# A slot-attention and mixture-of-experts kernel: scores ahead of the query turn, the slot sums' reciprocal behind the subtraction, four groups written out

## The chip, the cores and the metric

One core of a Trainium2 chip runs the whole kernel. The metric is the device time of one execution in microseconds (us). The engines are TensorE (PE; its weight loads are listed as PEld), VectorE (DVE), ScalarE (ACT), GpSimd (POOL) and SyncE (SP, which here only issues DMAs). Each engine runs its own list of instructions in order and waits for the others at semaphores.

## The reference

Cut to what matters. `x` is 32 batches of 56 slots with 128 features, `ctx` is 32 batches of 1500 tokens with 128 features.

```python
slots = layernorm(x)
Pn = rmsnorm(ctx, input_norm_w); k = Pn @ Wk.T; v = Pn @ Wv.T
for _ in range(3):
    q = rmsnorm(slots, slot_norm_w) @ Wq.T
    scores = einsum('bkd,bmd->bkm', q, k) * SCALE
    attn = softmax(scores, axis=-2)                      # over the 56 slots
    attn = attn / (attn.sum(-1, keepdims=True) + EPS)    # over the 1500 tokens
    slots = gru_cell(attn @ v, slots)
x = x + slots
x = x + top2_of_8_experts(layernorm(x))                  # each expert: gelu(x @ w1.T) @ w2.T
```

## The kernel before

The 32 batches are worked on in four groups of eight (`PAIR = 8`, `NPAIR = 4`). For a group there is an attention stage and then an expert stage. In the expert stage the context of the next group is also loaded, normalized, split into two fp16 parts (`ctx_rows`) and turned (`ctx_cols`). Ahead of the first group stands a prologue that does this for group 1, with the weights.

The attention stage has 24 steps (three iterations of eight batches), laid over 28 rounds (`ROUNDS`), n = 0 to 27. A step s is one batch in one iteration. Its work is spread over rounds:

- PE makes the scores of step n + 1 in round n (`scores`, L418: 12 chunks of 125 tokens by 3 products, 36 matmuls into one of two pairs of PSUM banks), and in round n the attention-weighted sums of step n - 3 (`update`, L431 and L436).
- DVE in round n takes the maximum over the slots of step n (L985), sums the exponentials of step n - 1 (L992), scales these sums (L1007) and takes their reciprocal `rden` (L1010), and then subtracts the maximum of step n from its scores (L1016), which is what ACT needs for the exponential of step n (L688).
- POOL multiplies the exponentials of step n - 1 with `rden` (L813). ACT casts the result of step n - 2 to fp16 (L674) and POOL makes the low half (L807), after which PE can run `update`.

Every second round one couple of batches (112 slots) also passes through the gated unit. In even rounds DVE normalizes the sums (L1030, L1033) and PE runs the gates (L457). In odd rounds ACT makes the gates (L663, L668) and the candidate (L684), DVE combines them (L999, L1003, L1021, L1027) into the new slots `h`. In even rounds the new slots make queries: ACT squares them (L608), PE forms the sum of squares and the query rows (`queries`, L399 and L400), ACT and POOL make the scale (L612, L772) and scale the rows (L617), and PE turns them (`turn_q`, L405). ACT and DVE write the two halves of the turned query, `qk` (L622, L890). The scores of an even step wait for that.

On PE a round of before has this order: `gates_of_slots` (L449), `queries`, `update`, `turn_q`, `scores`, then a slots' turn at the end of the stage, and `gates_of_updates` (L457). In rounds 0 to 2 there is no `update` yet.

In every engine's program a loop (`Fori`) runs the body for groups 1 to 3, and the body stands a second time for group 4, which has no next context to prepare. The loop's back edge is taken twice, at the end of groups 1 and 2. The last thing that PE does in a body of the loop is `scores` of step 0 of the next group, and a wait for the experts' last sum (`mixed`). SP's body begins with the loads of the next group's first three contexts and ends with the store of the group's output.

Of the kernel before, what the change touches and what calls it, by code (L numbers as in the profile page):

```python
# [14 lines left out]
TP = 125  # L15
TPE = TP + 1
CHUNKS = TOKENS // TP
# [33 lines left out]
def slot_attention_moe(nc, x, ctx, wq, wk, wv, wih, whh, bih, bhh, slot_w, input_w, router, w1, w2, out):  # L51
    with ExitStack() as stack:
# [227 lines left out]
        def _(sp):  # L280
            def load_ctx(j, b):
                r = b % RAW
                src = ctx[batch_of(j, b):batch_of(j, b) + 1] if isinstance(j, int) else ctx[bass.ds(batch_of(j, b), 1)]
                src = src.rearrange("o (p c) d -> p (o c) d", c=CHUNKS)

                if b >= RAW:
                    wait(sp, rows_ready, nth(j, PAIR, b - RAW + 1))
                elif not (isinstance(j, int) and j == 0):
                    wait(sp, rows_ready, nth(j, PAIR, b + RAW * (raw_uses(b) - 1) + 1 - PAIR))
                sp.dma_start(ctx_raw[0:XDMA_ROWS, r], src[0:XDMA_ROWS]).then_inc(ctx_loaded[r], DMA)  # L290
                sp.dma_start(ctx_raw[XDMA_ROWS:TP, r], src[XDMA_ROWS:TP]).then_inc(ctx_loaded[r], DMA)
# [4 lines left out]
            def rows_of(t, j):  # L296
                j8 = t[j * PAIR:(j + 1) * PAIR] if isinstance(j, int) else t[bass.ds(j * PAIR, PAIR)]
                return j8.rearrange("(t b) k d -> (b k) t d", b=2)

# [48 lines left out]

            with sp.Fori(0, NPAIR - 1) as i:
                body(i, True)  # L350
            body(NPAIR - 1, False)
            sp.wait_ge(out_stored, DMA * (NPAIR + 1))
# [3 lines left out]
        def _(pe):  # L356
# [50 lines left out]
            def scores(i, s):  # L407
                b, g = s % PAIR, (s // GROUP) % NG
                if s % GROUP == 0:
                    wait(pe, qk_ready, nth(i, GSTEPS, s // GROUP + 1))  # L410
                if s < PAIR:
                    wait(pe, cols_by_dve, nth(i, PAIR, b + 1))
                    wait(pe, cols_by_act, nth(i, 2 * PAIR, 2 * (b + 1)))
                wait_reuse(pe, shift_ready, i, STEPS, s - 1)
                for c in range(CHUNKS):
                    o = (c % HALF) * SLOTS
                    for n, (cp, qp) in enumerate(PRODUCTS):
                        mm = pe.matmul(score_ps[:, 2 * (s % 2) + c // HALF, o:o + SLOTS], ctx_cols[:, b, cp, c, :],  # L418
                                       qk[:, g, qp, (b % GROUP) * SLOTS:(b % GROUP + 1) * SLOTS],
                                       start=(n == 0), stop=(n == 2))  # L420
                mm.then_inc(scores_ready, 1)
# [104 lines left out]
            def body(i, more):  # L526
                for n in range(ROUNDS):
# [5 lines left out]
                    if LAG <= n < STEPS + LAG:  # L533
                        update(i, n - LAG)
                    if m is not None:
                        turn_q(i, m)
                    if n + 1 < STEPS:
                        scores(i, n + 1)
                    if tile_done_at(n) is not None and tile_done_at(n) < RT - 1:
# [35 lines left out]

            with pe.Fori(0, NPAIR - 1) as i:
                body(i, True)
            body(NPAIR - 1, False)

# [4 lines left out]
        def _(act):  # L584
# [151 lines left out]

            with act.Fori(0, NPAIR - 1) as i:
                body(i, True)
            body(NPAIR - 1, False)


        @block.gpsimd
        def _(pool):
# [83 lines left out]

            with pool.Fori(0, NPAIR - 1) as i:
                body(i, True)
            body(NPAIR - 1, False)  # L830


        @block.vector
        def _(dve):
# [142 lines left out]
            def body(i, more):  # L977
                chain.enter(PRO + i * PER)
                for n in range(ROUNDS):
# [15 lines left out]
                    if done is not None:  # L995
# [8 lines left out]
                            .then_inc(npre_ready, 1)  # L1004
                    if 0 <= s < STEPS:
                        wait(dve, den_ready, nth(i, STEPS, s + 1))
                        nc.vector.tensor_scalar(dup_ps, den_ps, 1.0 / ATTN_UP, None, ALU.mult).then_inc(den_scaled, 1)  # L1007
                        wait(dve, den_scaled, nth(i, STEPS, s + 1))
                        wait_reuse(dve, soft_ready, i, STEPS, s - 1)
                        nc.vector.reciprocal(rden[0:TP, s % 2], dup_ps).then_inc(rden_ready, 1)  # L1010
                    if n < STEPS:
# [4 lines left out]
                        nc.vector.tensor_tensor(soft[0:TP, n % 4].rearrange("p (h c) k -> p h c k", h=2), banks,  # L1016
                                                tops, ALU.subtract).then_inc(shift_ready, 1)
                    if done is not None:

# [4 lines left out]
                    if done is not None:  # L1024
                        wait(dve, cand_scaled, nth(i, GSTEPS, done + 1))
                        wait(dve, zh_ready, nth(i, GSTEPS, done + 1))
                        nc.vector.tensor_tensor(h[:, done % NG, :], zh[:, :], z_cand_home(done), ALU.subtract).then_inc(h_ready, 1)  # L1027
                    if gs is not None:
                        wait(dve, upd_ready, nth(i, STEPS, GROUP * (gs + 1)))
# [52 lines left out]

            with dve.Fori(0, NPAIR - 1) as i:
                body(i, True)
            body(NPAIR - 1, False)


# [24 lines left out]
```

## Time and profile before

| | us |
|---|---|
| median of 3 runs | 862.6 |
| lowest and highest run | 862.13 and 865.19 |
| profiled execution | 859.8 |
| its span, first to last instruction | 857.9 |
| prologue | 0 to 79.5 |
| attention rounds, group 1 | 79.5 to about 195 |
| first maximum (L985) of groups 2, 3 and 4 at | 282.3, 491.4, 697.3 |

How to read the rows: times are us from the start of the span. A line of the timeline has the start, the duration, the engine, the line of the kernel, the operation, output and inputs, and how many instructions were merged. In square brackets stands how long the engine was idle before it, and who released it; "issue" there means that nothing the profile shows was waited for. Within one engine, an instruction can start a little before the one ahead of it has ended.

### The profile page before, as it was taken

To read this page: it belongs to the slowest core of one execution; us is meant where nothing else is said; L and a number is where in the kernel's file an instruction comes from. 1 tells how busy PE (TensorE), PEld (TensorE's weight loads), DVE (VectorE), ACT (ScalarE), POOL (GpSimd) and SP (SyncE) were. 2 spreads that over 40 slices of the span, in tenths; PEclk is the share of its full clock that TensorE was granted. 3 is DMA by queue.
4 is the path that set the end of the run, shared out by engine and by line. 5 is a ranking of instruction groups with operands and counts; after the bars stand their busy time and mean duration, and the time that the engine had idled before them with its cause. 6 is when DMAs were issued, how large, how long until landed. Compare 5 with 4: busy or idle time off the path is not lost.

```text
span 857.9 us, 31055 instructions
## 1 busy us (share of the span) xinstructions
PE 662.3 (77%) x12876; PEld 571.3 (67%) x12876; DVE 685.1 (80%) x1406; ACT 526.1 (61%) x1048; POOL 529.2 (62%) x446
## 2 busy tenths in 40 slices
PE   2656899958676499985767569998676859998697
PEld 1545899845555499984556569997364659998476
DVE  5786899977986499996979559998697869999476
ACT  3664566648676256664858436666576755666375
POOL 5973787884574177878465237888565717787300
PEclk9767799988998599998989869999698989999799
DMA  8754000001310400000221130000031100000000
GB/s 176 182 146 134 3 4 3 4 12 42 102 41 2 122 3 4 3 4 11 74 72 38 38 85 4 3 5 3 12 108 37 38 12 3 5 3 3 2 2 12
DMA packets 15456, 33.45 MB, mean 39 GB/s; under 512 B 1411, under 2 KB 10259, under 8 KB 15307
## 3 DMA queue, kind: packets, MB, share of 16 engines
q1 hardware_dynamic: 15307, 31.36, 14.0%
q8 instruction: 107, 1.75, 0.8%
q14 instruction: 42, 0.34, 0.1%
HBM read 30.29 MB, written 0.92 MB: 36 GB/s over the span
## 4 chain that ended last, share of the span: by engine, by line
issue 31%; PE 25%; POOL 20%; DVE 18%; ACT 4%; DMA 2%; SPq 1%; POOLq 0%; ACTq 0%; DVEq 0%
POOL ctx_raw L755 8%; POOL ctx_rstd L753 7%; PE score_ps L418 5%; PE upd_ps L431 5%; DVE soft L1016 4%; DVE score_ps L992 3%; PE upd_ps L436 3%; PE score_ps L478 3%; PE score_ps L465 2%; DVE top L985 2%; PE gru_ps L399 2%; PE gru_ps L400 2%; DVE qk L890 1%; POOL attn L807 1%; DMA soft<-in_L_ffn_w_dram 1%
## 5 line engine op out<-in xcount | busy, mean ns | idle before, releaser
L807 POOL TENSOR_TENSOR attn<-soft,attn 125x672 f16<-125x672 f32 x96 | 140.6, 1464 | 29.5 <-ACT attn L674 28.6
L478 PEld LDWEIGHTS score_ps<-w_t,hidden 128*128 128x128 f16 x1536 | 103.6, 104 | 59.4 <-DVE hidden L1052 37.3
L813 POOL TENSOR_TENSOR soft<-soft,rden 125x672 f32<-125x672 f32 x96 | 126.0, 1312 | 24.3 <-DVE rden L1010 24.3
L478 PE MATMUL score_ps<-w_t,hidden 128*128 128x128 f16 x1536 | 116.8, 231 | 28.9 <-DVE hidden L1052 28.9
L1052 DVE TENSOR_TENSOR hidden<-hid,hidden 128x448 f16<-128x448 f32 x128 | 99.4, 785 | 48.2 <-ACT hidden L702 47.6
L418 PE MATMUL score_ps<-qk,ctx_cols 128*128 128x56 f16 x3456 | 113.5, 192 | 10.5 <-DVE qk L890 5.6
L755 POOL TENSOR_TENSOR ctx_raw<-ctx_raw,ctx_rstd 125x1536 f32<-125x1536 f32 x32 | 116.9, 3652 | 2.5
L418 PEld LDWEIGHTS score_ps<-qk,ctx_cols 128*128 128x128 f16 x3456 | 106.4, 99 | 12.6 <-issue 9.8
L985 DVE TENSOR_REDUCE top<-score_ps 125x12 f32<-125x672 f32 x96 | 81.9, 853 | 38.7 <-PE score_ps L418 33.6
L431 PE MATMUL upd_ps<-attn,ctx_rows 126*128 126x56 f16 x3456 | 108.1, 189 | 3.3 <-POOL attn L807 3.0
L465 PE MATMUL score_ps<-ycols,w_t 128*128 128x448 f16 x384 | 105.4, 393 | 5.1 <-ACT hid L707 5.1
L431 PEld LDWEIGHTS upd_ps<-attn,ctx_rows 126*128 126x128 f16 x3456 | 105.4, 97 | 5.5 <-POOL attn L807 4.9
L688 ACT ACTIVATE soft<-soft 125x672 f32<-125x672 f32 x96 | 73.2, 762 | 52.9 <-DVE soft L1016 50.4
L370 PE MATMUL upd_ps<-ident,ctx_rows 128*128 128x128 f16 x768 | 70.5, 250 | 43.1 <-DVE ctx_rows L847 30.0
L370 PEld LDWEIGHTS upd_ps<-ident,ctx_rows 128*128 128x128 f16 x768 | 56.7, 114 | 51.8 <-issue 19.4
L992 DVE TENSOR_REDUCE score_ps<-soft 125x12 f32<-125x672 f32 x96 | 81.7, 851 | 1.5 <-ACT soft L688 1.4
L674 ACT CAST attn<-soft 125x672 f16<-125x672 f32 x96 | 71.5, 744 | 16.4 <-POOL soft L813 14.4
L593 ACT CAST ctx_rows<-ctx_raw 125x1536 f16<-125x1536 f32 x32 | 47.3, 1478 | 51.3 <-POOL ctx_raw L755 51.3
L707 ACT ACTIVATE hid<-score_ps 128x448 f32<-128x448 f32 x128 | 69.7, 548 | 12.6 <-PE score_ps L465 12.3
L1016 DVE TENSOR_TENSOR soft<-score_ps,top 125x672 f32<-125x672 f32 x96 | 76.8, 800 | 0.5
L436 PE MATMUL upd_ps<-attn,ones 126*128 126x56 f16 x2304 | 76.5, 188 | 0.0
L753 POOL TENSOR_TENSOR ctx_rstd<-ctx_ms,mhalf 125x12 f32<-125x12 f32 x32 | 72.7, 2272 | 2.6 <-POOL ctx_ms L752 0.2
(127 smaller groups left out, 1220.1 us busy)
## 6 DMA issues: line engine op xcount, KB each, us to landing
ctx_raw<-in_ctx_dram SPq DMA_DIRECT2D x32, 672.0 KB
soft<-in_L_ffn_w_dram SPq DMA_DIRECT2D x16, 256.0 KB, 5.0
ctx_raw<-in_ctx_dram SPq DMA_DIRECT2D x32, 78.0 KB
x_in<-in_x_dram SPq DMA_DIRECT2D x4, 224.0 KB, 2.7
out_dram<-acc SPq DMA_DIRECT2D x4, 224.0 KB, 3.2
soft<-in_L_xattn_gru_wih_dram SPq DMA_DIRECT2D x1, 192.0 KB, 3.6
soft<-in_L_xattn_gru_whh_dram SPq DMA_DIRECT2D x1, 192.0 KB, 3.8
ctx_rows<-hidden SPq DMA_DIRECT2D x1, 144.0 KB
```

The source lines that it names most:

```text
L370: mm = pe.transpose(bank[:, k * D:(k + 1) * D], ctx_rows[:, b, part, c, :], ident16[:, :])
L418: mm = pe.matmul(score_ps[:, 2 * (s % 2) + c // HALF, o:o + SLOTS], ctx_cols[:, b, cp, c, :], qk[:, g, qp, (b % GROUP) * SLOTS:(b % GROUP ...
L431: pe.matmul(upd_ps[:, gs % 2, o:o + SLOTS], ctx_rows[0:TPE, b, cp, c, :], attn[0:TPE, s % 3, ap, c, :], start=(c == 0 and n == 0), stop=(c ...
L436: mm = pe.matmul(upd_ps[:, gs % 2, GW + o:GW + o + SLOTS], ones16[0:TPE, :], attn[0:TPE, s % 3, ap, c, :], start=(c == 0 and ap == HI), st ...
L465: mm = pe.matmul(score_ps[:, n % 2, 0:PW], w1_t[:, wp, e, c * D:(c + 1) * D], ycols16[:, yp, :], start=(k == 0), stop=(k == 2))
L478: mm = pe.matmul(score_ps[:, 2 + e % 2, t * D:(t + 1) * D], hidden[:, n % HRING, hp, t * ROWS:t * ROWS + D], w2_t[:, wp, e, c * D:(c + 1) ...
L753: chain.link(nc.gpsimd.tensor_tensor(ctx_rstd[0:TP, r], ctx_ms[0:TP, r], mhalf[0:TP, :], ALU.pow))
L755: nc.gpsimd.tensor_tensor(rows, rows, ctx_rstd[0:TP, r].unsqueeze(2).to_broadcast([TP, CHUNKS, D]), ALU.mult).then_inc(ctx_scaled, 1)
L807: nc.gpsimd.tensor_tensor(attn[0:TP, s % 3, LO], soft[0:TP, s % 4], attn[0:TP, s % 3, HI], ALU.subtract).then_inc(attn_ready, 1)
L813: nc.gpsimd.tensor_tensor(a, a, rden[0:TP, s % 2].unsqueeze(2).to_broadcast([TP, CHUNKS, SLOTS]), ALU.mult).then_inc(soft_ready, 1)
L992: nc.vector.tensor_reduce(den_ps, soft[0:TP, s % 4], AX_X, ALU.add).then_inc(den_ready, 1)
L1016: nc.vector.tensor_tensor(soft[0:TP, n % 4].rearrange("p (h c) k -> p h c k", h=2), banks, tops, ALU.subtract).then_inc(shift_ready, 1)
```

## The change

Three edits.

- The loops over the groups are written out: each engine's body is emitted four times with constant addresses and semaphore values.
- On PE, `scores` of step n + 1 is issued ahead of `turn_q`, behind `update`. For steps 3 and up `scores` now waits for `rden_ready` of step s - 3 and not for `shift_ready` of step s - 2. Both come from DVE's round s - 2, where the reciprocal now stands behind the subtraction, and the reciprocal's input lies in the same pair of banks.
- On DVE, the subtraction L1016 goes ahead of the scaling L1007 and of the reciprocal L1010. The scaling follows right behind it, and the reciprocal stands behind the two operations that finish the slots (L1021, L1027).

```diff
@@ PE, scores
-                wait_reuse(pe, shift_ready, i, STEPS, s - 1)
+                if s >= 3:
+                    wait(pe, rden_ready, nth(i, STEPS, s - 2))
+                else:
+                    wait_reuse(pe, shift_ready, i, STEPS, s - 1)
@@ PE, round
+                    if n + 1 < STEPS:
+                        scores(i, n + 1)
                     if m is not None:
                         turn_q(i, m)
-                    if n + 1 < STEPS:
-                        scores(i, n + 1)
@@ DVE, round
-                    if 0 <= s < STEPS:
-                        wait(dve, den_ready, nth(i, STEPS, s + 1))
-                        nc.vector.tensor_scalar(dup_ps, den_ps, 1.0 / ATTN_UP, None, ALU.mult).then_inc(den_scaled, 1)
-                        wait(dve, den_scaled, nth(i, STEPS, s + 1))
-                        wait_reuse(dve, soft_ready, i, STEPS, s - 1)
-                        nc.vector.reciprocal(rden[0:TP, s % 2], dup_ps).then_inc(rden_ready, 1)
                     if n < STEPS:
...
                                                 tops, ALU.subtract).then_inc(shift_ready, 1)
+                    if 0 <= s < STEPS:
+                        wait(dve, den_ready, nth(i, STEPS, s + 1))
+                        nc.vector.tensor_scalar(dup_ps, den_ps, 1.0 / ATTN_UP, None, ALU.mult).then_inc(den_scaled, 1)
                     if done is not None:
...
                         nc.vector.tensor_tensor(h[:, done % NG, :], zh[:, :], z_cand_home(done), ALU.subtract).then_inc(h_ready, 1)
+                    if 0 <= s < STEPS:
+                        wait(dve, den_scaled, nth(i, STEPS, s + 1))
+                        wait_reuse(dve, soft_ready, i, STEPS, s - 1)
+                        nc.vector.reciprocal(rden[0:TP, s % 2], dup_ps).then_inc(rden_ready, 1)
@@ every engine (here PE)
-            with pe.Fori(0, NPAIR - 1) as i:
-                body(i, True)
-            body(NPAIR - 1, False)
+            for i in range(NPAIR):
+                body(i, i < NPAIR - 1)
```

## Rows read from the trace of the kernel before

**Rows 1.** The page: busy time by engine, and a DMA queue (packets, MB).

```profile
PE 662.3 (77%) x12876; PEld 571.3 (67%) x12876; DVE 685.1 (80%) x1406; ACT 526.1 (61%) x1048; POOL 529.2 (62%) x446
q8 instruction: 107, 1.75, 0.8%
```

**Rows 2.** Stretches: length, busy time per engine (PE, PEld, DVE, ACT, POOL), clock, DMA share, GB/s.

```profile
79.50:100.00 20.50, 15.45 (x321) 14.26 (x320) 14.22 (x26) 8.94 (x20) 10.16 (x10) 0.67 0.13 37
282.30:308.50 26.20, 16.13 (x321) 14.77 (x321) 14.19 (x26) 9.23 (x21) 10.13 (x10) 0.61 0.36 93
491.40:516.50 25.10, 15.90 (x322) 14.65 (x322) 14.26 (x27) 9.24 (x21) 10.22 (x10) 0.66 0.36 95
697.30:716.30 19.00, 12.66 (x321) 11.69 (x321) 14.25 (x27) 8.75 (x20) 10.13 (x10) 0.91 0.05 14
...
107.50:155.40 47.90, 45.73 (x1274) 43.55 (x1269) 45.91 (x105) 31.92 (x79) 39.04 (x38) 1.00 0.01 4
```

**Rows 3.** Timeline of DVE: an odd round's maximum, then the next odd round.

```profile
108.02 0.86 DVE L985 TENSOR_REDUCE top<-score_ps 125x12 f32<-125x672 f32 x1
...
115.80 0.85 DVE L985 TENSOR_REDUCE top<-score_ps 125x12 f32<-125x672 f32 x1
...
118.10 0.17 DVE L1007 TENSOR_SCALAR score_ps<-score_ps 125x12 f32<-125x12 f32 x1
...
118.30 0.23 DVE L1010 RECIPROCAL rden<-score_ps 125x12 f32<-125x12 f32 x1
118.45 0.79 DVE L1016 TENSOR_TENSOR soft<-score_ps,top 125x672 f32<-125x672 f32 x1
...
119.16 0.27 DVE L1021 SCALAR_TENSOR_TENSOR upd_ps<-z_gate,upd_ps 128x112 f32<-128x112 f32 x1
...
119.46 0.27 DVE L1027 TENSOR_TENSOR h<-zh,upd_ps 128x112 f32<-128x112 f32 x1
```

**Rows 4.** Timeline of PE and DVE at the end of the next, even, round.

```profile
121.72 0.78 PE L436 MATMUL upd_ps<-attn,ones 126*128 126x56 f16 x24
...
122.48 0.32 PE L405 MATMUL gru_ps<-ident,q_rows 112*128 112x112 f32 x1
...
122.63 1.09 PE L418 MATMUL score_ps<-qk,ctx_cols 128*128 128x56 f16 x36
...
123.43 0.27 DVE L1033 TENSOR_TENSOR upd<-upd_ps,inv_sum 128x112 f32<-128x112 f32 x1
...
123.76 0.92 PE L457 MATMUL gru_ps<-upd,wx_t 128*128 128x112 f32 x6
123.77 0.86 DVE L985 TENSOR_REDUCE top<-score_ps 125x12 f32<-125x672 f32 x1
```

**Rows 5.** Timeline of ACT and POOL between the two.

```profile
118.47 0.35 ACT L684 ACTIVATE upd_ps<-npre,vec 128x112 f32<-128x112 f32 x1
118.64 1.46 POOL L807 TENSOR_TENSOR attn<-soft,attn 125x672 f16<-125x672 f32 x1 [0.22 <-ACT attn L674]
...
119.95 0.28 ACT L608 ACTIVATE h_sq<-h 128x112 f32<-128x112 f32 x1
120.06 1.31 POOL L813 TENSOR_TENSOR soft<-soft,rden 125x672 f32<-125x672 f32 x1
```

**Rows 6.** Timeline of PE across the back edge into group 2.

```profile
279.71 1.09 PE L418 MATMUL score_ps<-qk,ctx_cols 128*128 128x56 f16 x36
284.70 0.53 PE L399 MATMUL gru_ps<-ones,h_sq 128*112 128x1 f32 x2 [3.89 <-issue]
...
291.15 1.00 PE L418 MATMUL score_ps<-qk,ctx_cols 128*128 128x56 f16 x18 [2.64 <-issue]
```

**Rows 7.** Timeline of the first rounds of group 4: a turn, two maxima.

```profile
699.22 0.31 PE L405 MATMUL gru_ps<-ident,q_rows 112*128 112x112 f32 x1 [1.38 <-ACT q_rows L617]
...
700.51 0.86 DVE L985 TENSOR_REDUCE top<-score_ps 125x12 f32<-125x672 f32 x1 [1.49 <-PE score_ps L418]
...
708.82 0.86 DVE L985 TENSOR_REDUCE top<-score_ps 125x12 f32<-125x672 f32 x1 [2.37 <-PE score_ps L418]
```

More of the change, by code:

```diff
@@ L282, in load_ctx @@
                 r = b % RAW
-                src = ctx[batch_of(j, b):batch_of(j, b) + 1] if isinstance(j, int) else ctx[bass.ds(batch_of(j, b), 1)]
-                src = src.rearrange("o (p c) d -> p (o c) d", c=CHUNKS)
+                src = ctx[batch_of(j, b):batch_of(j, b) + 1].rearrange("o (p c) d -> p (o c) d", c=CHUNKS)
                 if b >= RAW:
                     wait(sp, rows_ready, nth(j, PAIR, b - RAW + 1))
-                elif not (isinstance(j, int) and j == 0):
+                elif j > 0:
                     wait(sp, rows_ready, nth(j, PAIR, b + RAW * (raw_uses(b) - 1) + 1 - PAIR))
@@ L296, in rows_of @@
             def rows_of(t, j):
-                j8 = t[j * PAIR:(j + 1) * PAIR] if isinstance(j, int) else t[bass.ds(j * PAIR, PAIR)]
-                return j8.rearrange("(t b) k d -> (b k) t d", b=2)
+                return t[j * PAIR:(j + 1) * PAIR].rearrange("(t b) k d -> (b k) t d", b=2)
             load_ctx(0, 0)
@@ L347, in body @@
                 sp.dma_start(rows_of(out, i), acc[:]).then_inc(out_stored, DMA)
-            with sp.Fori(0, NPAIR - 1) as i:
-                body(i, True)
-            body(NPAIR - 1, False)
+            for i in range(NPAIR):
+                body(i, i < NPAIR - 1)
             sp.wait_ge(out_stored, DMA * (NPAIR + 1))
@@ L574, in body @@
                     wait(pe, mixed, nth(i, EXPERTS, EXPERTS))
-            with pe.Fori(0, NPAIR - 1) as i:
-                body(i, True)
-            body(NPAIR - 1, False)
+            for i in range(NPAIR):
+                body(i, i < NPAIR - 1)
         EXP_TANH = "exp_and_others"
@@ L735, in body @@
                         copy_turned(i + 1, PAIR - 1, t)
-            with act.Fori(0, NPAIR - 1) as i:
-                body(i, True)
-            body(NPAIR - 1, False)
+            for i in range(NPAIR):
+                body(i, i < NPAIR - 1)
         @block.gpsimd
@@ L826, in body @@
                             rstd_rows(nth(i + 1, LNT_PER, RT))
-            with pool.Fori(0, NPAIR - 1) as i:
-                body(i, True)
-            body(NPAIR - 1, False)
+            for i in range(NPAIR):
+                body(i, i < NPAIR - 1)
         @block.vector
@@ L1081, in body @@
                             qk_lo(i + 1, 0)
-            with dve.Fori(0, NPAIR - 1) as i:
-                body(i, True)
-            body(NPAIR - 1, False)
+            for i in range(NPAIR):
+                body(i, i < NPAIR - 1)
 _INS = ['x', 'ctx_1024', 'L0_xattn_Wq', 'L0_xattn_Wk', 'L0_xattn_Wv', 'L0_xattn_gru_wih', 'L0_xattn_gru_whh',
```

## The prediction

> **What bounds the kernel now.** I read the page first, then stretches, then the chain of waits for their order, and the timeline round by round. DVE is the busiest engine over the span [rows 1], but an average over stages decides nothing. In steady attention rounds DVE is busy for 45.91 of 47.90 us, PE for 45.73, POOL for 39.04 and ACT for 31.92, at full granted clock (1.00, which is 2.4 GHz) [rows 2]. DVE and PE are thus both close to full, and what sets the time is a loop through both. The chain of waits passes, for every couple of batches, from DVE's subtraction and the new slots (L1016, L1021, L1027) over ACT's square (L608) to PE's queries, the update (L431, L436) and then either DVE's L1030 and L1033 or PE's turn and scores (L405, L418), to the next maximum L985. Two such turns take from 108.02 to 123.77, so 7.88 us for one pair of rounds [rows 3, 4].
>
> The first rounds of a group are another matter. From the first maximum to the sixth they take 20.50, 26.20, 25.10 and 19.00 us in the four groups, and DVE is busy for only 14.2 of them each time [rows 2]. Two things stand out. In groups 2 and 3, which are entered by the loop's back edge, 6 to 7 us more pass than in group 4, which isn't. And in group 4 too DVE waits for scores that stand behind a query turn [rows 7].
>
> **Part 1, the loops written out.** At the back edge PE has finished its scores at 280.80 (279.71 + 1.09) and begins its next instruction at 284.70, 3.89 us idle of which nothing is released by another engine; within the scores of step 1 it stops again for 2.64 us [rows 6]. With constant addresses there is no jump, so both should go. How much of it reaches the end is best read from whole starts. From the last matmul of the first scores to the sixth maximum, groups 1 and 4, entered straight, need about 20.5 and 19.0 us: the stretches of rows 2 begin within 0.1 us of that matmul. Groups 2 and 3 need their 26.2 and 25.1 plus the 1.5 us (280.80 to 282.30) by which DVE too starts late at the back edge [rows 2, 6]; for group 3 I take the same 1.5. If they become like group 1 the gain is 7.2 + 6.1 = 13.3 us; like group 4, 8.7 + 7.6 = 16.3. Group 4's clock in this stretch is 0.91, against 0.67 in group 1, and its DMAs are few (0.05 against 0.13), while groups 2 and 3 load contexts there (0.36) [rows 2]. I take the middle, 15.
>
> The stop inside the scores could also be put down to those loads and not to the jump. Then the 2.64 us stay in both groups, 5.3 us, and part 1 brings 9.7. The rows lean to the jump, since the stop comes in PE's first matmuls behind it and group 1, which loads as well, shows no such stall in its 20.50 us. The Trainium skill (Runtime: NRT & Kernel Launch, Instruction fetch mechanics) says that instructions are fetched in blocks of 16 KiB one ahead of the other, and that a taken branch to a target outside the two blocks held forces a fetch before execution goes on. By that rule the stop goes too and part 1 is worth its full 15; by the reading from the loads it would be 9.7. The queue's 107 packets of 1.75 MB [rows 1] agree with 16 KiB each.
>
> The longer programs cost nothing that I can find: they execute the same instructions, and in the steady rounds, where nothing is loaded, the DMAs still move 4 GB/s [rows 2], so instructions are being fetched while they run, loop or not. On SP the loads of the next contexts go out about 1 us earlier, with nothing queued that is needed before round 24; should they disturb, it is the 5.3 us above.
>
> **Part 2, scores ahead of the turn, in the first rounds.** In round 0, and in the same way in round 2, PE stands 1.38 us before the turn, waiting for ACT's scaled rows, while the next scores, whose query has long been there, are queued behind it; DVE then waits 1.49 us for the maximum of step 1 and 2.37 us for that of step 3 [rows 7]. Now those scores run in that gap. They need 1.1 us at full clock [rows 4], so the first turn, before at 699.22, is hardly later (scores could start at 697.84, 1.38 ahead, and end at 698.9). Its query is as early as before. The maximum of step 1 comes 1.5 us earlier. With it the subtraction, the exponential and, queued behind that on ACT, the square for the next query come earlier, and in round 2 the wait for the scores of step 3 goes as well: 1.49 + 2.37 = 3.9 us is the most. The turn of step 3's neighbour then lands behind the scores, and update 0 waits for POOL, whose line L813, ACT's cast, L807 starts only with the first reciprocal. That gives some back, about 1 us. The least is 1.5 (only the first gap). I take 2.9 for each group, nearer the top, because both waits have the same cause: 4 x 2.9 = 11.6 us.
>
> **Part 3, steady rounds.** In an odd round L1016 takes the place of L1007 and starts at 118.10, not 118.45. It ends at 118.89. L1007 (0.17, overlapping by 0.08 as independent DVE instructions do here: 118.45 against 118.53) ends at 118.99, L1021 follows from 118.91 and L1027 from 119.21 to 119.48, where it ended at 119.73: 0.25 us earlier, since the 0.23 us reciprocal has left this path [rows 3]. L1021 needs ACT's candidate, ready at 118.82 [rows 5], so it just isn't held. L608 started 0.22 after the slots at 119.95 [rows 5], and PE's queries and update end 0.25 earlier with it, and so do L1030 and L1033. The turn used to stand between L436's end at 122.50 and the scores, which ended at 123.72, just ahead of L985 at 123.77 [rows 4]. With the turn (0.3) behind the scores they end about 0.2 + 0.25 earlier, so DVE's side is the later: L1033 ended at 123.70 and L985 can overlap it by 0.08. It starts 0.25 + 0.15 = 0.40 earlier in this pair of 7.97, and 0.25 in the other of the two, which has 7.78 (15.75 - 7.97) and no wait for scores. That is 0.33 on average, and 7.55 a pair.
>
> Is the moved work covered? The turn now ends at about 123.4 of the old times; L457 behind it waits for L1033 anyway, and ACT's L622 has until DVE has done the next L985. The reciprocal of the odd round ends at about 119.63, against 118.53; behind it waits POOL's L813, which started only at 120.06, held by L807 until 120.10 [rows 5]. The cover is 0.43 us and is what I trust least: if the candidate came later by more than that, L813 would move. The new wait of the scores on `rden_ready` concerns the DVE round before. PE gets to the even round's scores at 122.3, 2.7 us behind that reciprocal. It holds nothing. In even rounds the reciprocal ends as before, 0.1 us sooner.
>
> There are nine such pairs from the sixth maximum to the 24th in each group, so 36 x 0.33 = 12 us. An alternative value comes from the other end: nothing at all if POOL or ACT close the loop in DVE's stead (0), or 0.5 us a pair (18) if scores too drew everything forward. The expert stage and the last four rounds see neither edit: 0.
>
> **Sum.** 15 + 11.6 + 12 = 38.6, say 39 us. From the profiled execution, 859.8 (span 857.9 and 1.9 around it), this leaves 820.8. That execution lies 2.8 us below the median of the runs, 862.6, to which the forecast refers: 862.6 - 39 = 823.6.
>
> **The rivals.**
>
> - The steady rounds don't gain. POOL's multiplication and subtraction (1.31 and 1.46 us [rows 5]) follow each other through ACT's cast, twice a pair, and the late reciprocal uses up its cover. For it: POOL already has 39.04 busy of 47.90 [rows 2], 6.4 us of each pair, with the casts' gaps on top; against it: the 0.43 us of cover. 39 - 12 = 27 gives 835.6.
> - More than forecast: groups 2 and 3 start like group 4, PE's clock stays up in the shorter first rounds, 3.9 us each in part 2 and 0.4 a pair: 16.3 + 15.6 + 14.4 = 46, 816, and down to 810 with 0.5 a pair.
> - Only the loops: the first rounds are given back at once because POOL's line sets the sixth maximum, and the steady rounds stay. 15 alone gives 847.6, and 853 if the stop in the scores stays too.
> - Slower: written out, PE's stream stalls where it runs straight. The place is a block boundary, 107 of them [rows 1], the price that of the stop seen, 2.64 us [rows 6], and it decides from 15 such stops (39 / 2.64). With 25 it would be 890. Against it: the loop's body is itself a long straight line, and in its steady rounds PE is busy 45.73 of 47.90 [rows 2].
> - The change doesn't do what it says: PE has its weight load ahead and gains nothing by the swap. It is part of the third rival, since the 1.38 us before the turn is a real wait for ACT.
>
> **How the numbers follow.** Forecast, 817 to 831: 0.55. Steady rounds without gain, 831 to 843: 0.20. More than forecast, 808 to 817: 0.10. Only the loops, 843 to 858: 0.08. No change: 0.03. Slower: 0.04. The range 809 to 843 leaves out the last three and a little at the bottom, 0.16 to 0.18. A difference under 0.5%, 4.3 us, is about what a measurement of this kernel can't tell from none. Faster 0.93, same 0.03, slower 0.04.
>
> **What would show it.** In the changed kernel PE's idle "issue" of 3.89 and 2.64 us at the starts of groups 2 and 3 is gone (part 1). The first to the sixth maximum take about 16 to 17.5 us in every group (parts 1 and 2), and L418 runs ahead of L405. Pairs of rounds take about 7.55 us, L608 starts 3.9 us after the odd round's L985 and not 4.15, and L813 has no idle time released by L1010 in steady rounds (part 3). The prediction is wrong if L813 shows such waits of over 0.4 us, if pairs stay at 7.8, or if PE's stops for "issue" turn up in the middle of rounds.

## The result and the profile after

The changed kernel takes 824.8 us (median of four runs, 821.59 to 826.13). The runs of before that stand beside it have a median of 863.89. The ratio is 0.953, with a 95% interval of 0.9475 to 0.9586. The forecast was 823.6, in a range of 809 to 843. The profiled execution took 824.36 us with a span of 822.6, which is 35.3 less than the 857.9 of before.

In the changed kernel the maximum is L982, the sum of exponentials L989, the subtraction L1007, the scaling L1011, the reciprocal L1025 and the slots' two operations L1015 and L1021. ACT's candidate is L683 and its square L607, PE's turn is L402, and POOL's two operations are L811 and L805. PE's scores and update keep their lines. First the page: the busy time by engine, and the queue of PE's instructions.

```profile
PE 653.0 (79%) x12876; PEld 565.9 (69%) x12876; DVE 677.9 (82%) x1406; ACT 528.8 (64%) x1048; POOL 522.9 (64%) x446
q8 instruction: 101, 1.65, 0.8%
```

The same work now lies in a shorter span [rows 1]. Next, stretches of the changed kernel, in the columns of rows 2: from the first to the sixth maximum in each group, and steady rounds of group 1.

```profile
80.38:96.12 15.74, 12.17 (x321) 11.24 (x320) 13.86 (x26) 8.51 (x19) 9.34 (x9) 0.89 0.16 44
275.87:292.90 17.03, 13.56 (x321) 12.63 (x321) 13.87 (x27) 8.53 (x20) 10.09 (x10) 0.80 0.58 151
470.49:489.06 18.57, 15.10 (x321) 14.17 (x321) 13.90 (x27) 8.53 (x20) 10.08 (x10) 0.72 0.55 139
665.45:683.83 18.38, 14.91 (x321) 13.97 (x321) 13.90 (x27) 8.53 (x20) 10.09 (x10) 0.72 0.06 15
...
107.50:155.40 47.90, 46.73 (x1336) 45.06 (x1336) 47.02 (x109) 33.64 (x84) 40.79 (x40) 1.00 0.02 4
```

Against [rows 2] the starts are shorter by 4.8, 9.2, 6.5 and 0.6 us. In the steady rounds DVE is now busy for 47.02 of 47.90 us. The starts (from the first to the sixth maximum of a group) get longer as their granted clock falls from 0.89 to 0.72, and PE is busy in them for 12.17 us in the shortest and 15.10 in the longest. Their DVE time is the same in all four.

Now the timeline of one steady odd round, all engines, answering [rows 3] and [rows 5].

```profile
126.23 0.85 DVE L982 TENSOR_REDUCE top<-score_ps 125x12 f32<-125x672 f32 x1
...
128.53 0.85 DVE L1007 TENSOR_TENSOR soft<-score_ps,top 125x672 f32<-125x672 f32 x1
...
128.90 0.35 ACT L683 ACTIVATE upd_ps<-npre,vec 128x112 f32<-128x112 f32 x1
129.07 1.47 POOL L805 TENSOR_TENSOR attn<-soft,attn 125x672 f16<-125x672 f32 x1 [0.21 <-ACT attn L673]
129.29 0.17 DVE L1011 TENSOR_SCALAR score_ps<-score_ps 125x12 f32<-125x12 f32 x1
129.37 0.27 DVE L1015 SCALAR_TENSOR_TENSOR upd_ps<-z_gate,upd_ps 128x112 f32<-128x112 f32 x1
129.41 0.77 ACT L687 ACTIVATE soft<-soft 125x672 f32<-125x672 f32 x1 [0.16 <-DVE soft L1007]
...
129.67 0.27 DVE L1021 TENSOR_TENSOR h<-zh,upd_ps 128x112 f32<-128x112 f32 x1
129.86 0.23 DVE L1025 RECIPROCAL rden<-score_ps 125x12 f32<-125x12 f32 x1
130.00 0.79 DVE L982 TENSOR_REDUCE top<-score_ps 125x12 f32<-125x672 f32 x1
130.08 0.28 ACT L607 ACTIVATE h_sq<-h 128x112 f32<-128x112 f32 x1
...
130.49 1.31 POOL L811 TENSOR_TENSOR soft<-soft,rden 125x672 f32<-125x672 f32 x1
```

ACT's square starts 3.85 us after the odd round's maximum (4.15 before). It stands right behind ACT's exponential L687, which ends at 130.18, and not right behind the slots, which are ready at 129.94. The kernel before has the same order. There the slots were ready at 119.73, but ACT was in its exponential until 120.04, and the square started at 119.95 [rows 5]:

```profile
119.28 0.76 ACT L688 ACTIVATE soft<-soft 125x672 f32<-125x672 f32 x1 [0.46 <-DVE soft L1016]
```

What brings the square forward by 0.30 us is thus the subtraction, which releases the exponential. The reciprocal ends at 130.09 and POOL takes it at 130.49, behind its own L805. The cover is thus 0.40 us and was not used up. The even round that follows, PE and DVE, answers [rows 4].

```profile
131.85 0.78 PE L436 MATMUL upd_ps<-attn,ones 126*128 126x56 f16 x24
...
132.47 1.09 PE L418 MATMUL score_ps<-qk,ctx_cols 128*128 128x56 f16 x36
...
133.41 0.29 PE L402 MATMUL gru_ps<-ident,q_rows 112*128 112x112 f32 x1
133.56 0.27 DVE L1031 TENSOR_TENSOR upd<-upd_ps,inv_sum 128x112 f32<-128x112 f32 x1
133.76 0.85 DVE L982 TENSOR_REDUCE top<-score_ps 125x12 f32<-125x672 f32 x1
```

The scores end at 133.56, ahead of the 133.83 of DVE's L1031, so it is DVE that decides when the next maximum starts. From 126.23 to 133.76 the pair takes 7.53 us.

The table has all kernels that the rest speaks of. "Starts" is the time from first to sixth maximum in groups 1 to 4, "pair" the mean of eight steady pairs (sixth to 22nd maximum) in group 1, with other groups where they differ from it by more than 0.05. Both are read from one profiled execution. A single start can differ by over 1 us where the engines have the same to do: in group 1 it takes 15.7 us in the changed kernel at a clock of 0.89, and 17.2 at 0.80 in e11, where only the loads are moved.

| kernel | median | span | starts, groups 1 to 4 | pair |
|---|---|---|---|---|
| before | 862.6 | 857.9 | 20.5, 26.2, 25.1, 19.0 | 7.89 |
| changed | 824.8 | 822.6 | 15.7, 17.0, 18.6, 18.4 | 7.53 |
| e1 loops written out only | 847.3 | 843.3 | 19.3, 19.3, 19.9, 18.9 | 7.89 |
| e2 both orders, loops kept | 842.8 | 841.5 | 18.2, 25.6, 26.9, 17.2 | 7.52 |
| e3 loops out, PE's order | 840.5 | 832.5 | 17.5, 17.6, 17.8, 17.5 | 7.83 |
| e4 loops out, DVE's order | 837.7 | 837.1 | 20.0, 19.3, 18.2, 20.2 | 7.74 |
| e5 before, late loads | 868.9 (one run) | 867.0 | 20.8, 22.6, 23.0, 19.0 | 8.44, 8.39, 8.44, 7.89 |
| e6 changed, filler | 819.5 | 815.9 | 15.4, 16.0, 17.3, 17.0 | 7.52 |
| e7 changed, reciprocal early | 831.1 | 830.7 | 17.2, 18.5, 17.1, 18.5 | 7.70 |
| e11 changed, loads spaced | 822.9 | 820.8 | 17.2, 17.3, 18.6, 18.4 | 7.53 (group 2: 7.60) |
| e12 changed, loads bunched | 838.1 | 837.1 | 18.2, 17.3, 18.3, 17.2 | 8.00, 8.22, 8.12, 7.52 |
| e8 filler and spaced loads | 820.8 | 816.9 | 15.4, 16.7, 17.0, 16.8 | 7.52 |
| e9 the same, filler in round 3 too | 815.3 | 812.5 | 15.4, 15.4, 15.4, 15.4 | 7.52 (groups 2, 3: 7.63, 7.58) |

Runs of before that shared the chip had medians of 865.2 (e1 to e4), 864.8 (e5 to e7) and 862.1 (e8 to e12).

### The profile page after: what moved, and what is told of

It is laid out like the page before. It is cut to its first block, busy times and chain, and to the rows that moved or that the text cites. A ratio compares the mean times of both kernels' runs of the same rounds, so it can differ in the third digit from the quotient of the medians.

```text
span 822.6 us, 29805 instructions
## 1 busy us (share of the span) xinstructions
PE 653.0 (79%) x12876; PEld 565.9 (69%) x12876; DVE 677.9 (82%) x1406; ACT 528.8 (64%) x1048; POOL 522.9 (64%) x446
## 4 chain that ended last, share of the span: by engine, by line
DVE 47%; PE 19%; issue 13%; POOL 9%; ACT 9%; DMA 2%; SPq 1%; POOLq 0%; DVEq 0%; ACTq 0%
DVE score_ps L989 7%; DVE inv_sum L1028 5%; DVE hidden L1050 4%; PE score_ps L478 4%; DVE soft L1007 4%; DVE top L982 4%; DVE ctx_rows L844 4%; POOL ctx_raw L753 4%; PE score_ps L465 3%; DVE ssq L840 3%; PE upd_ps L367 3%; POOL ctx_rstd L751 2%; DVE rden L1025 2%; PE upd_ps L431 2%; ACT hid L706 2%
## 5 line engine op out<-in xcount | busy, mean ns | idle before, releaser
L805 POOL TENSOR_TENSOR attn<-soft,attn 125x672 f16<-125x672 f32 x96 | 140.6, 1465 | 29.9 <-ACT attn L673 28.9
L1050 DVE TENSOR_TENSOR hidden<-hid,hidden 128x448 f16<-128x448 f32 x128 | 101.1, 801 | 49.1 <-ACT hidden L701 48.8
L811 POOL TENSOR_TENSOR soft<-soft,rden 125x672 f32<-125x672 f32 x96 | 126.1, 1314 | 14.9 <-DVE rden L1025 14.6
L418 PE MATMUL score_ps<-qk,ctx_cols 128*128 128x56 f16 x3456 | 110.0, 190 | 4.1 <-DVE qk L887 3.9
L753 POOL TENSOR_TENSOR ctx_raw<-ctx_raw,ctx_rstd 125x1536 f32<-125x1536 f32 x32 | 110.8, 3463 | 2.5
L418 PEld LDWEIGHTS score_ps<-qk,ctx_cols 128*128 128x128 f16 x3456 | 101.8, 98 | 5.3 <-DVE qk L887 4.6
L982 DVE TENSOR_REDUCE top<-score_ps 125x12 f32<-125x672 f32 x96 | 79.4, 827 | 13.2 <-PE score_ps L418 13.2
L687 ACT ACTIVATE soft<-soft 125x672 f32<-125x672 f32 x96 | 73.1, 762 | 15.4 <-DVE soft L1007 15.4
L989 DVE TENSOR_REDUCE score_ps<-soft 125x12 f32<-125x672 f32 x96 | 81.5, 849 | 0.5
L1007 DVE TENSOR_TENSOR soft<-score_ps,top 125x672 f32<-125x672 f32 x96 | 81.4, 848 | 0.3 <-issue 0.2
```

The lines of the kernel that those rows point to most:

```text
L753: nc.gpsimd.tensor_tensor(rows, rows, ctx_rstd[0:TP, r].unsqueeze(2).to_broadcast([TP, CHUNKS, D]), ALU.mult).then_inc(ctx_scaled, 1)
L805: nc.gpsimd.tensor_tensor(attn[0:TP, s % 3, LO], soft[0:TP, s % 4], attn[0:TP, s % 3, HI], ALU.subtract).then_inc(attn_ready, 1)
L811: nc.gpsimd.tensor_tensor(a, a, rden[0:TP, s % 2].unsqueeze(2).to_broadcast([TP, CHUNKS, SLOTS]), ALU.mult).then_inc(soft_ready, 1)
L982: nc.vector.tensor_reduce(top[0:TP, n % 2], banks, AX_X, ALU.max).then_inc(max_ready, 1)
L989: nc.vector.tensor_reduce(den_ps, soft[0:TP, s % 4], AX_X, ALU.add).then_inc(den_ready, 1)
L1050: nc.vector.tensor_tensor(hidden[:, k % HRING, LO, 0:PW], hid32[:, k % GRING, :], hidden[:, k % HRING, HI, 0:PW], ALU.subtract).then_inc(h ...
```

## The experiments

### Which part brings what: e1 to e4

**e1: the loops written out, nothing else.**

```diff
-            with pe.Fori(0, NPAIR - 1) as i:
-                body(i, True)
-            body(NPAIR - 1, False)
+            for i in range(NPAIR):
+                body(i, i < NPAIR - 1)
```

> The kernel before with only its loops written out; both orders stay. Theory (the back edge costs about 15 us in the starts of groups 2 and 3, nothing elsewhere): first to sixth maximum of groups 2 and 3 at 19 to 20.5 us instead of 26.2 and 25.1, groups 1 and 4 and the steady pairs (7.88 us) unchanged, no idle of 3.89 or 2.64 us for issue; 862.6 - 15 = about 848. Rival A (the stop within the scores comes from the context loads): it stays at 2.6 us in groups 2 and 3, 853. Rival B (the loops are worth more, since the measured starts of the changed group 4 gained only 0.6 us): 840 or less.

Measured: 847.3 us, ratio 0.9797 (0.9766 to 0.9828). The span is 14.6 us shorter than before, pairs are at 7.89, and the starts of groups 2 and 3 are 6.9 and 5.2 us shorter. No stop for issue is left in the starts. That much of the theory holds. Of the 14.6 us, however, only 12.1 lie in the starts of groups 2 and 3. Another 1.6 come from a shorter prologue and 1.2 from the start of group 1, neither of which the back edge touches (in the other kernels with written out loops the first maximum stands at 79.1 to 81.5 us, before it stood at 79.5). The time from the 24th maximum of a group to the next group's first maximum is not shorter: 111.7 and 112.4 us for groups 1 and 2, against 111.5 and 112.1.

**e2: both orders, the loops kept.** The edit is the change's own diff without its last part.

> The changed kernel with the loops kept, so both orders without the writing out. Theory (the parts add up): steady pairs at 7.53 us, 12 us from them, and 2 to 3 us from each start; the stops for issue stay; 862.6 - 12 - 10 = about 840. Rival (behind the back edge PE fetches late, so that scores ahead of the turn gain nothing in groups 2 and 3): 845.

Measured: 842.8, ratio 0.9737 (0.9704 to 0.9769). Pairs are at 7.52, so the whole steady gain comes from the orders. The starts of groups 1 and 4 are shorter than before, but those of groups 2 and 3 are 25.6 and 26.9. Behind the back edge the orders bring nothing. The view of waits tells why:

```profile
PE score_ps L421 <- issue: 10.4, 2, 6.0
PE gru_ps L399 <- issue: 7.4, 2, 3.9
```

These are sum, number and longest. The stop within the first scores, 2.64 us before [rows 6], is now up to 6.0. PE gets to the point sooner, and its instructions are not there sooner. The rival's mechanism was right. Its 845 was not reached, since groups 1 and 4 and the pairs gained.

**e3: loops written out, scores ahead of the turn; DVE as before.**

```diff
-                    if m is not None:
-                        turn_q(i, m)
                     if n + 1 < STEPS:
                         scores(i, n + 1)
+                    if m is not None:
+                        turn_q(i, m)
```

> Loops written out and on PE the scores ahead of the turn, DVE's order as before (reciprocal ahead of the subtraction, scores waiting for the subtraction as before). Theory: the starts gain as in the changed kernel, and of the steady pair only the 0.15 to 0.2 us by which the scores came late in every second pair, so pairs of about 7.78; 4 x 9 x 0.1 = 3.6 of the 12.4 us; about 824.8 + 9 = 834. Rival (DVE's order brings nothing without this one and this one brings all): pairs of 7.53, 825.

Measured: 840.5, ratio 0.9732 (0.9675 to 0.9789), 6.5 above the 834 expected, with runs spread over 11 us. The profiled span of 832.5 lies at the low end of them, so I go by the trace, and what made the other runs longer isn't shown. Starts are 17.5 to 17.8, on average 1.8 us shorter than e1's. Their sum is 70.4, against 69.7 in the changed kernel, so nearly the whole gain of the starts comes from PE's order. Pairs are at 7.83, only 0.06 under e1's, and not at the 7.78 expected.

**e4: loops written out, the subtraction first on DVE; PE as before.** The edit is the change's part on DVE, with the scores' new wait.

> Loops written out and on DVE the subtraction first, the turn still ahead of the scores. Theory: new slots 0.25 us earlier in the odd round, but scores behind the turn then end last: pair 7.97 - 0.25 = 7.72, the starts as in the kernel before (20.5 to 19 us): 848 - 6 = about 842. Rival (the parts don't need each other): pair 7.63.

Measured: 837.7 (842 was expected), ratio 0.9664 (0.9616 to 0.9712). Pairs are at 7.74, against 7.72 expected. Starts are as in e1 (sum 77.7 against 77.5).

Together e3 and e4 say what the change's two orders do in the steady pair. PE's alone brings 0.06 us, DVE's alone 0.15, both 0.36. The two paths into the next maximum (DVE's sums, or PE's turn and scores) end nearly together in the kernel before. Shortening one leaves the other in charge, and only both together give the whole.

### What the place of the reciprocal is worth: e7

```diff
                         nc.vector.tensor_scalar(dup_ps, den_ps, ...).then_inc(den_scaled, 1)
+                        wait(dve, den_scaled, nth(i, STEPS, s + 1))
+                        wait_reuse(dve, soft_ready, i, STEPS, s - 1)
+                        nc.vector.reciprocal(rden[0:TP, s % 2], dup_ps).then_inc(rden_ready, 1)
...
-                    if 0 <= s < STEPS:
-                        wait(dve, den_scaled, nth(i, STEPS, s + 1))
-                        wait_reuse(dve, soft_ready, i, STEPS, s - 1)
-                        nc.vector.reciprocal(rden[0:TP, s % 2], dup_ps).then_inc(rden_ready, 1)
```

> The changed kernel with the reciprocal right behind the scaling, so ahead of the slots' last two operations, both still behind the subtraction. Theory (0.25 us of the pair come from the reciprocal having left the path to the new slots): slots 0.23 us later, ACT's square held by them rather than by its exponential, pair 7.72 to 7.76; 36 x 0.21 = 7.6 us more, 832. Rival (what counts is the subtraction ahead of both, which starts the exponential): pair 7.53 to 7.58, 825 to 827.

Measured: 831.1, ratio 0.9616 (0.9567 to 0.9665), pairs 7.70. In the timeline of e7's odd round the reciprocal (here L1015) stands ahead of the slots (L1019, L1025), and now it is the slots that ACT's square waits for:

```profile
128.17 0.84 DVE L982 TENSOR_REDUCE top<-score_ps 125x12 f32<-125x672 f32 x1
...
131.34 0.76 ACT L687 ACTIVATE soft<-soft 125x672 f32<-125x672 f32 x1 [0.16 <-DVE soft L1007]
131.43 0.23 DVE L1015 RECIPROCAL rden<-score_ps 125x12 f32<-125x12 f32 x1
131.58 0.26 DVE L1019 SCALAR_TENSOR_TENSOR upd_ps<-z_gate,upd_ps 128x112 f32<-128x112 f32 x1
131.87 0.27 DVE L1025 TENSOR_TENSOR h<-zh,upd_ps 128x112 f32<-128x112 f32 x1
...
132.18 0.30 ACT L607 ACTIVATE h_sq<-h 128x112 f32<-128x112 f32 x1
```

The square starts 4.01 us after the maximum, against 3.85 in the changed kernel and 4.15 before. The reciprocal behind the slots is worth 0.17 us of a pair, 36 x 0.17 = 6 us, and 6.3 is the difference of the medians. The subtraction ahead of both brings the rest of the 0.36, so it does not do it alone. The theory's 0.21 was a little high. The slots come 0.26 us later (3.97 after the maximum, against 3.71), but in the changed kernel they were ready 0.14 us before the square, which stood behind the exponential. Only the remainder reaches the square.

### Where the stop within the scores came from: e5, e12, e11

**e5: the kernel before, with the loads moved.**

```diff
                 if more:
+                    wait(sp, h_ready, nth(i, GSTEPS, NG))
                     for b in range(RAW):
                         load_ctx_next(i, b)
```

The first four couples' slots are ready in round 11, so the loads come in the middle of the steady rounds.

> The kernel before, loop and orders as they are, but SP issues the next group's first three context loads only when four couples of slots are done in round 11, so that no loads run at a group's start. Theory (the stop of 2.64 us within the scores of step 1 comes from the jump): it is there in groups 2 and 3 as before, and first to sixth maximum stay at 25 to 26 us there. Rival (it comes from the loads): the stop goes, the starts shorten to 23.5 or less, while the 3.89 us at the back edge stay.

Measured: 868.9 in one run, beside a median of 864.8 of before. One run says little of the time, so I go by its trace. The stop of 2.64 us is gone: the scores of step 1 of group 2 run in one piece.

```profile
285.38 1.09 PE L419 MATMUL score_ps<-qk,ctx_cols 128*128 128x56 f16 x36
289.65 0.53 PE L400 MATMUL gru_ps<-ones,h_sq 128*112 128x1 f32 x2 [3.18 <-ACT h_sq L609]
...
292.41 1.89 PE L419 MATMUL score_ps<-qk,ctx_cols 128*128 128x56 f16 x36
```

The gap at the back edge stays (285.38 + 1.09 = 286.47 to 289.65). Starts fall to 22.6 and 23.0, as the rival said (23.5 or less). What I had not expected is in the table: the pairs of the groups that load rise from 7.89 to about 8.4, 4.0 to 4.4 us for each group. PE stops for issue in the middle of an update, in code with no jump near:

```profile
347.31 0.42 PE L432 MATMUL upd_ps<-attn,ctx_rows 126*128 126x56 f16 x10
350.26 1.37 PE L432 MATMUL upd_ps<-attn,ctx_rows 126*128 126x56 f16 x26 [2.53 <-issue]
```

So the loads can stop PE anywhere, and not only behind a jump. e5 still had a loop, and the next two runs take it away.

**e12: the changed kernel, its three loads issued together behind the subtraction of step 7. e11: the same loads, one each behind steps 7, 11 and 15.**

```diff
 # e12
+                    wait(sp, shift_ready, nth(i, STEPS, 8))
                     for b in range(RAW):
                         load_ctx_next(i, b)
 # e11
                     for b in range(RAW):
+                        wait(sp, shift_ready, nth(i, STEPS, 8 + 4 * b))
                         load_ctx_next(i, b)
```

> The changed kernel with the same three loads issued together behind the subtraction of step 7, in the middle of the steady rounds. Theory: instruction blocks wait for all three loads, PE stops for issue for 2 to 3 us or more in each of groups 1 to 3, some 4 us of steady time each as in the loop kernel with late loads; 825 + 12 = 837. Rival (a straight program has fetched far enough ahead, only a program with a loop stops): 825, no stops.

> The changed kernel, but SP issues the next group's first three context loads one at a time, behind the subtractions of steps 7, 11 and 15 and not together at the group's start. Theory (no block of PE's instructions arrives while context loads fill the queues; three together last over 10 us, one alone about 3.5 us, which PE's stock of fetched instructions covers): no idle for issue in the steady rounds, pairs 7.53 in all groups, time as the changed kernel, 825. Rival (any load in the steady rounds stops PE): three stops in each of groups 1 to 3, pairs of 7.7 or more, 835 or more.

Measured: e12 838.1, ratio 0.9705 (0.9653 to 0.9757), e11 822.9, ratio 0.9539 (0.9493 to 0.9586), against 0.953 for the changed kernel. Stretches of 4 us in group 2 of e12, and PE's timeline just behind:

```profile
309.00:313.00 4.00, 4.00 (x121) 3.92 (x118) 3.93 (x11) 2.62 (x8) 3.42 (x5) 1.00 0.63 168
313.00:317.00 4.00, 3.80 (x120) 3.63 (x117) 3.93 (x8) 3.18 (x9) 3.23 (x4) 1.00 0.99 259
317.00:321.00 4.00, 2.43 (x54) 2.26 (x51) 3.33 (x10) 2.65 (x7) 3.64 (x4) 1.00 0.62 159
...
322.55 0.72 PE L432 MATMUL upd_ps<-attn,ctx_rows 126*128 126x56 f16 x12 [3.12 <-issue]
```

While the DMA share is 0.99, PE runs on. Then it stops, 2.2, 3.1 and 3.6 us in groups 1 to 3, once in each. A program without a loop does it too, and the same bytes spaced out leave one stop of 0.34 us in the whole kernel. Theory confirmed on both sides.

That PE lacks instructions in these stops is not only inferred. The trace holds the transfers of the queue q8, which brings PE's instructions in pieces of 16384 bytes. In the steady rounds of the changed kernel one starts about every 4.5 us. In e12 one starts at 309.95, and the next only at 319.85, as the loads end. It has landed at 321.12, and PE goes on at 322.55. The same holds for all 20 stops for issue of over 0.3 us that PE has in the traces of before, e2, e5, e6, e9, e11 and e12: each ends 1.2 to 1.7 us after such a piece has landed.

A stop costs more than its own length. Behind it PE runs at 1.2 GHz for a while (granted clock 0.50 from 322.5 to 328.0), and 36 matmuls of scores take 1.86 us and not 1.09.

```profile
324.20 1.86 PE L419 MATMUL score_ps<-qk,ctx_cols 128*128 128x56 f16 x36
```

From the sixth to the 24th maximum the three groups take 3.8, 5.3 and 4.8 us more than in the changed kernel.

### Why the starts differ: e6, e8, e9

In the changed kernel the 36 matmuls of one step's scores take 1.10 us in rounds 0 and 1 of group 4, and 1.89 in round 2, after PE has stood idle for 0.95 and 1.40 us:

```profile
668.70 1.10 PE L418 MATMUL score_ps<-qk,ctx_cols 128*128 128x56 f16 x36 [0.95 <-DVE qk L887]
...
671.20 0.53 PE L396 MATMUL gru_ps<-ones,h_sq 128*112 128x1 f32 x2 [1.40 <-ACT h_sq L607]
...
672.14 1.89 PE L418 MATMUL score_ps<-qk,ctx_cols 128*128 128x56 f16 x36
```

**e6: matmuls that nobody reads, in those gaps.** Their result goes to a bank that the first update overwrites. e8 has the loads of e11 as well, and e9 has 20 more in round 3.

```diff
+                    if n == 2:
+                        filler(i, 36)      # ahead of queries
...
+                    if n == 0:
+                        filler(i, 20)      # behind turn_q
```

> The changed kernel with matmuls whose result nobody uses in PE's idle times of the first rounds: 20 behind the turn of round 0 and 36 ahead of the queries of round 2 (0.6 and 1.1 us at full clock, less than the idle times of 0.95 and 1.40 us). Theory (groups 2 to 4 lose 1.3 to 2.8 us against group 1 because the granted clock falls to half, 1.2 GHz, behind these idle times): every group's first to sixth maximum at 15.7 us or less, clock about 1.00 there; 824.8 - 6.7 = 818. Rival (the clock falls whatever stands in these gaps, or the filler stands in the way): 825 to 830, starts of 17 to 19 us.

> The changed kernel with the filler matmuls in the first rounds (20 and 36) and the context loads spaced as in the run before. Theory (the filler holds the clock, and its stops of 1.7 and 0.4 us for issue in groups 3 and 2 came from the loads at the group's start): starts of 15.4 us in all groups, 819.5 - 2.5 = 817. Rival (the stops come from the filler's own instructions): stops of the same size stay, 819.5.

> As the run before, with 20 more filler matmuls ahead of the first update in round 3, where PE was idle for 0.83 us. Theory (a longer unbroken run of work holds the clock in group 4 too, which fell to 0.90): 15.2 to 15.4 us in every group, 816. Rival (the first update is held by POOL, the filler changes nothing or is in the way): 817 to 818.

Measured: e6 819.5 (0.9507, 0.9449 to 0.9564), e8 820.8 (0.9517, 0.9473 to 0.9561), e9 815.3 (0.9453, 0.9404 to 0.9503). Of e6's starts only that of group 1 is at the 15.7 or less that was expected for all. The clock is 1.00 in groups 1 to 3, but 0.90 in group 4, and groups 2 and 3 pay 0.37 and 1.70 us of stops for issue, since the filler's instructions too have to come through the loads. Spacing the loads removed these stops (e8), but groups 2 to 4 all fell to 0.90, so nothing was won: the theory for e8 missed by 4 us. Why groups 2 and 3 kept the clock in e6 and not in e8 isn't shown. Only e9 held the clock everywhere. Its starts, in the columns of rows 2:

```profile
79.97:95.38 15.41, 13.11 (x397) 12.35 (x396) 13.82 (x27) 8.27 (x19) 9.20 (x9) 1.00 0.01 3
272.48:287.90 15.42, 13.25 (x397) 12.49 (x397) 13.80 (x26) 8.15 (x19) 9.19 (x9) 1.00 0.07 18
466.07:481.51 15.44, 13.26 (x397) 12.49 (x397) 13.81 (x26) 8.14 (x19) 9.19 (x9) 1.00 0.08 19
658.30:673.73 15.43, 13.25 (x397) 12.49 (x397) 13.82 (x26) 8.16 (x19) 9.19 (x9) 1.00 0.07 18
```

All four are alike within 0.03 us, with 76 matmuls more than the changed kernel executes there. The starts' sum is 61.7 us against 69.7. e9 is the fastest of all kernels here. Its interval overlaps those of e6 and of the changed kernel, so by the medians alone the lead over the changed kernel is not beyond doubt; the spans, 812.5 against 822.6, differ by the 8.0 us of the starts and 2 us elsewhere.

## Why the prediction was right, and where it was not

**Part 3, the steady rounds (12 us forecast): right in size, with one link of the chain misread.** From the sixth to the 24th maximum the four groups together take 12.4 us less. The pair came out at 7.53 for 7.55, and L607 at 3.85 for 3.9. e3 and e4 show that both orders are needed. The cover of 0.43 us for the late reciprocal was 0.40. No wait of POOL for the reciprocal is left in steady rounds: the page's four such waits are one for each group, at its first step. The rival without steady gain is out. But the 0.25 us by which queries, update and sums should come earlier were derived from the slots ("L608 started 0.22 after the slots"), and in both kernels the square stands behind ACT's exponential. Counted from the odd round's maximum, the subtraction ends 0.29 us earlier than before, the exponential and the square start 0.30 earlier, and the slots are ready only 0.22 earlier. Moving the reciprocal pays because without it the slots would become the later of the two, as they do in e7. That 0.25 stood so close to 0.30 was in part luck.

**Part 1, the loops (15 us forecast): the mechanism held, the cause of one term was wrong, and the size was met in part by luck.** e1's span is 14.6 us shorter, but the starts of groups 2 and 3 give 12.1 of it. The forecast also counted 1.5 us twice for DVE's late start. That delay is gone in e1 (the first maximum of group 2 follows the scores within 0.1 us), but the stage before it took 1.6 us longer, and the difference was made up by the prologue and group 1. The step that gave the 2.64 us stop to the jump, "the rows lean to the jump", failed. e5 kept the jump and moved the loads, and the stop went. e1 removed the jump and kept the loads, and it went too. It takes both. In before a piece of PE's instructions lands at 283.02, the next, with the loads under way, only at 289.64, and PE goes on with the scores at 291.15. I had reasoned from group 1, "which loads as well". Its three loads were issued at 69.6 to 77.1 us, ahead of its first maximum at 79.5, and its first rounds have a DMA share of 0.13 [rows 2]. So it was no counterexample. The 3.89 us gap at the back edge is the jump's: e2, which keeps it, still has two of up to 3.9.

**Part 2, scores ahead of the turn at the starts (4 x 2.9 = 11.6 us forecast): the term that was mis-sized.** From e1 to the changed kernel the starts give 3.6, 2.3, 1.3 and 0.5 us, together 7.7. The second maximum comes at 1.67 us for the 3.2 of group 4 before, which is the first gap in full, and the fourth at 8.6 for 11.6. What the sum left out is the clock. In group 4 of the changed kernel PE is idle for 0.95 and 1.40 us, and then runs at 1.2 GHz (granted clock 0.50 from 671.2 to 679.0); over the whole start the clock is 0.72, where it was 0.91 before. With the clock held (e9) the fourth maximum comes at 7.6, and all starts are 15.4 us, 3.9 under e1's average of 19.4. That equals the upper bound of the prediction (3.9), but e1's own starts ran at 0.82 to 0.91, so some of it is clock that the order alone wouldn't give. Whether POOL takes back the "about 1 us" therefore stays open. The forecast took group 4's clock of 0.91 as given. e9 shows that it depends on PE's idle times, since filling three of them holds it. It is not shown why the new order keeps the clock low for longer: group 4 of before has idle times at the same two places, of 1.20 and 1.83 us, and still 0.91.

**The sum** lies 1.2 us from the median, closer than its parts. Between the two profiled executions the span falls by 35.3 us and not by 38.6: the starts give 21.1, the steady rounds 12.4, and the rest, 1.8, lies outside both, where nothing was forecast. The medians differ by 39.1 with the four runs that stand beside, and by 37.8 from the 862.6 that was shown, since the profiled execution of before, 859.8, was shorter than the three timed runs beside it. That part of the agreement is luck.

**The slower rival** (a straight stream that stops for issue) was given 0.04 and did not happen. But it is no fancy. e12 has stops of 2.2 to 3.6 us in straight code (without a loop), and is 13 us slower than the changed kernel by moving six DMA issues in each of three groups. The prediction's argument against it, that steady rounds show no such stop, held only because no loads ran in them.

The Trainium skill (Runtime: NRT & Kernel Launch, Instruction fetch mechanics) says that crossing from one block of instructions to the next is mostly hidden in straight code. Here that holds where the DMA share is 0.02 (no stop in the steady rounds of the changed kernel) and not where it is 0.99 (3.12 us in e12).

## What to carry to other kernels

- Where two engines' paths end nearly together in a loop, look for edits on both. Here 0.06 and 0.15 us alone made 0.36 together. What is not needed by the next step of the loop goes behind what is, as long as its own reader has cover: compare the two in the timeline.
- Large loads issued together delay the instruction stream of a busy TensorE. Put them where it executes little, or issue them one at a time.
- Where PE has little to do, read the granted clock before trusting matmul times. Matmuls that nobody reads, in the gaps and no longer than them, can hold it. Here 76 in three gaps did in every group (e9), 56 in two did not (e6, e8).
- Before you say what an operation waits for, look at its own engine too. Here the square came 0.22 us after the slots and was held by the exponential ahead of it on ACT.

## What the runs showed of the hardware that was not expected

- With a DMA share of 0.93 over 9.2 us (310.2 to 319.4 in e12), PE went on all that time and then stopped for 3.1 us, because no instructions had been brought in between 311.05 and 319.85. With one load of 750 KB at a time it stopped for at most 0.34 us (e11) and 0.62 (e9).
- After a back edge PE stood still for 3.9 us, and the orders' gain behind it was lost: the stop within the scores grew from 2.6 and 2.1 us to 4.4 and 6.0 (e2).
- Two independent DVE instructions overlap by 0.08 us (L1025 starts at 129.86, L1021 ends at 129.94), while one that waits for the other starts 0.03 us behind its end (L1021 at 129.67, L1015 until 129.64). The Trainium skill (VectorE: DVE Perf Modes, Rules for kernel authors) advises to count operations and not semaphores; here a wait on the DVE instruction just ahead costs 0.11 us, in rounds where DVE is busy for 47.02 of 47.90 us.
